# A gated cross-attention kernel: its first half regrouped into four phases a batch, with row-tiled transposes and another split of the PSUM reads

## The reference, cut to what matters

```python
xn   = layernorm(x)                                  # 32 x 112 x 256
qh   = split_heads(xn @ wq + bq)                     # 16 heads of 16
kh   = split_heads(ctx @ wk + bk);  vh = split_heads(ctx @ wv + bv)
attn = softmax(qh kh^T / 4 + mask * -1e9)            # 16 x 112 x 375
x    = x + tanh(g_xattn) * (merge(attn vh) @ wo + bo)
x    = x + tanh(g_ffn) * switch_attention(layernorm(x), ...)
```

## Time and profile before

| what | value |
|---|---|
| median of 3 runs | 1240.68 us (1239.48 to 1241.24) |
| profiled execution, its own time | 1238.06 us |
| its span, first to last instruction | 1236.3 us |
| PE, PEld busy | 96%, 77% of the span |
| DVE, ACT, POOL busy | 72%, 50%, 44% |
| DMA queue q1 | 71.1% of 16 engines' span |
| mean granted TensorE clock | 0.989 |

### The profile page before, as it was taken

One profiled execution on the slowest core, in us unless ns is written; L12 is line 12 of the kernel. 1 busy time (PEld: TensorE's weight loads), 2 busy tenths in 40 slices (PEclk: granted clock), 3 DMA queues, 4 the chain that ended last, 5 costly groups with the idle time before them and its releaser, 6 DMA issues. The chain is left out here.

```text
span 1236.3 us, 42159 instructions
## 1 busy us (share of the span) xinstructions
PE 1181.6 (96%) x16696; PEld 951.6 (77%) x16696; DVE 891.2 (72%) x2556; ACT 621.5 (50%) x1513; POOL 547.7 (44%) x821
## 2 busy tenths in 40 slices
PE   5799999999999999999879999999999999999975
PEld 4577777777777777777658888888888888888864
DVE  3577777777777777777666778777877877787752
ACT  3466666666666666666434444444444444444431
POOL 3476777777677777767610222122122212221210
PEclk9899999999999999999999999999999999999997
DMA  8898999788888778877316576666666665666663
GB/s 236 197 202 195 215 193 200 177 184 184 180 187 182 178 177 188 179 175 159 88 29 137 144 156 151 156 148 149 150 154 149 154 155 140 158 147 158 150 140 78
DMA packets 263011, 200.32 MB, mean 162 GB/s; under 512 B 195934, under 2 KB 243872, under 8 KB 258720
## 3 DMA queue, kind: packets, MB, share of 16 engines
q1 hardware_dynamic: 262816, 197.64, 71.1%
HBM read 125.49 MB, written 72.11 MB: 160 GB/s over the span
## 5 line engine op out<-in xcount | busy, mean ns | idle before, releaser
L899 POOL TENSOR_SCALAR shifted<-raw,neg_max 112x375 f32<-112x375 f32 x512 | 326.1, 645 | 164.9 <-DVE neg_max L781 121.1
L781 DVE CUSTOM_DVE_ANT_0 raw<-bank_s,maskb 112x375 f32<-112x375 f32 x512 | 266.6, 544 | 103.2 <-issue 88.1
L686 ACT ACTIVATE probsT<-bank_t 128x512 f32<-128x512 f32 (+3 forms) x512 | 189.2, 459 | 104.6 <-PE bank_t L460 104.6
L447 PE MATMUL bank_s<-K_stack,Q_stack 128*112 128x375 bf16 x512 | 151.1, 336 | 4.9 <-DVE neg_max L781 4.6
L460 PEld LDWEIGHTS bank_t<-ident,shifted 48*128 48x128 f32 (+1 forms) x3072 | 105.5, 139 | 28.0 <-issue 24.3
L203 POOL TENSOR_SCALAR var_eps<-moments 112x1 f32<-112x1 f32 x32 | 7.1, 223 | 261.1 <-DVE moments L199 260.9
L460 PE MATMUL bank_t<-ident,shifted 48*128 48x48 f32 (+1 forms) x3072 | 122.6, 226 | 0.2 <-issue 0.2
L1164 PE MATMUL bank_ab<-xnT,wq2T 128*128 128x224 f32 x512 | 109.5, 357 | 0.8 <-ACT qT L1365 0.6
L1164 PE MATMUL bank_ab<-xnT,wk2T 128*128 128x224 f32 x512 | 109.5, 357 | 0.0
L1476 DVE TENSOR_REDUCE max<-bank_s 112x4 f32<-112x448 f32 x128 | 78.8, 615 | 40.5 <-PE bank_s L1213 40.5
L1509 DVE COPY uT<-bank_g 64x192 f32<-64x192 f32 (+1 forms) x128 | 49.8, 389 | 80.6 <-PE bank_g L1263 79.3
(11 more groups left out here) (148 smaller groups left out, 2189.9 us busy)
## 6 DMA issues: line engine op xcount, KB each, us to landing
K_stack<-k_dram SPq DMA_DIRECT2D x64, 562.5 KB, 7.8
k_dram<-k_parts SPq DMA_DIRECT2D x32, 562.5 KB, 4.3
att_dram<-att_q SPq DMA_DIRECT2D x31, 511.0 KB, 3.3
att_th<-att_dram SPq DMA_DIRECT2D x31, 511.0 KB, 4.4
v_dram<-mv SPq DMA_DIRECT2D x32, 455.0 KB, 6.6
v<-v_dram SPq DMA_DIRECT2D x32, 455.0 KB, 4.5
K_stack<-k_dram SPq DMA_DIRECT2D x32, 375.0 KB, 9.3
Q_stack<-q_dram SPq DMA_DIRECT2D x64, 168.0 KB, 9.2
```

Of the source, the lines that this page charges most:

```text
L447: nc.tensor.matmul(bank_s[h % 2][0:S, 0:S2], Q_stack[:, p, h, :], K_stack[:, p, h, :], start=True, stop=True).then_inc(scores_ready, 1)
L686: act.activation(probsT[:, g % 2, first_u:end, lo:hi], bank_t[0:KP, bank, column:column + (end - first_u) * (hi - lo)].rearrange("p (u q) ...
L781: dve.tensor_tensor_reduce(raw[:, g % 2, j, :], bank_s[h % 2][0:S, 0:S2], c.maskb[:, :], -1.0, -LEAST, ALU.add, ALU.min, neg_max[:, g % 2, ...
L899: pool.tensor_scalar(shifted[:, g % 2, j, 0:S2], raw[:, g % 2, j, :], -1.0, neg_max[:, g % 2, j:j + 1], ALU.mult, ALU.add).then_inc(shift_ ...
```

## The change: what it does

- **Phases.** A batch is four phases of the same form: four scores with ordinary matmuls between them, then a `turn`, then a `weigh`. `turn` lies one group behind the scores and `weigh` one behind `turn`. Context and x are now turned for batch b+3, at the end of batch b.
- **Row-tiled turning.** The four small kinds of transposes are split as `turn` is: 64 rows each, half 0 to bank 0 and half 1 to bank 1 of `bank_ab` (`turn_halves`). They stand right behind a `turn`: `heads_back` behind the second, `heads_turn` behind the third, context and x behind the fourth. `xn`, `heads`, `xnT` and `outT` grow to 128 rows; POOL clears the tails once (`tails_set`). The heads come out in another order, so `wo` is loaded by four DMAs in that order.
- **Rests from PSUM.** ACT writes only the first part of k and q. DVE computes the rest straight from PSUM (`key_rest`, a half of k at a time, `query_rest`, two pieces), before PE may write that bank again. ACT makes the second key part in halves, POOL the third in halves. The scale 1/4 is put into `wq` once, in `prepare`.
- **Copies shared.** Context and turned x are copied out of PSUM by ACT (bank 0) and DVE (bank 1) at once.
- **Exchange.** Three query parts are stored, once; `Q_stack` is loaded by four DMAs. Queries are stored before keys. x is loaded one batch at a time.

The diff, cut to its core:

```diff
-STACKED = ((0, 3, 1), (3, 3, 2), (6, 2, 0))
+K_STACKED = ((0, 3, 0), (3, 3, 0), (6, 2, 0))
+Q_STACKED = ((0, 1, 2), (1, 2, 0), (3, 2, 0), (5, 3, 0))
...
+                sp.wait_ge(q_split, b + 1)
+                sp.dma_start(by_partition(q_dram[bass.ds(b, 1)]), q_parts[:, :, :, :]).then_inc(q_stored[p], 16)
+                sp.wait_ge(k_split, EC * (b + 1))
                 sp.dma_start(by_partition(k_dram[bass.ds(b, 1)]), k_parts[:, p, :, :, :]).then_inc(k_stored[p], 16)
...
+            def turn_halves(columns, width, src, f):
+                for r in range(2):
+                    rows = slice(r * HALF, (r + 1) * HALF)
+                    last = nc.tensor.transpose(bank_ab[0:f.stop - f.start, r, columns:columns + width], src[rows, f], c.ident[rows, rows])
+                return last
...
+            def body(b):
+                S_(b, 4, 5)
+                if b + 2 < B:
+                    keys(b + 2, 0, 0)
+                S_(b, 6)
+                if b + 2 < B:
+                    queries(b + 2)
...
+                S_(b, 7)
+                turn(b, 0, b == 0)
                 if back:
                     weigh(b - 1, 1 - p, NG - 1, False)
+                S_(b, 8, 9)
+                if b + 2 < B:
+                    keys(b + 2, 1, 0)
+                S_(b, 10, 11)
+                turn(b, 1, b == 0)
                 if back:
+                    if b + 2 < B:
+                        pe.wait_ge(k_rest_done, EC * (b + 3))
+                        pe.wait_ge(q_rest_done, EC * (b + 3))
...
                     heads_back(b - 1)
+                weigh(b, p, 0, b == 0)
+                S_(b, 12, 13)
+                if b + 1 < B:
...
                     values(1 - p, 0)
                     values(1 - p, 1).then_inc(va_ready, 1)
+                S_(b, 14, 15)
+                turn(b, 2, False)
+                if back:
...
+                    heads_turn(b - 1)
+                weigh(b, p, 1, False)
+                S_(b + 1, 0, 1)
+                if b + 1 < B:
...
+                    values(1 - p, 2).then_inc(vb_ready, 1)
                 else:
+                    open_proj(0)
+                S_(b + 1, 2)
+                if back:
+                    project(b - 1)
+                S_(b + 1, 3)
+                if b + 1 == B:
+                    open_proj(1)
+                turn(b, 3, False)
+                if b + 3 < B:
+                    turn_ctx(b + 3)
+                    turn_x(b + 3)
...
+                weigh(b, p, 2, False)
...
+            def key_rest(b, p, t, bank):
+                dve.wait_ge(k_copied, EC * b + t + 1)
...
+                dve.scalar_tensor_tensor(k_rest[:, t, :], bank_ab[:, bank, 0:S2], c.bk[:, t:t + 1], k_parts[:, p, 0, t, :],
+                                         ALU.add, ALU.subtract).then_inc(k_rest_done, 1)
...
+            def body(b):
+                score_max(b, b == 0, 4, 5)
+                if x_next < 0:
+                    moments_of(b + 3)
...
+                score_max(b, b == 0, 6)
+                if b + 2 < B:
+                    key_rest(b + 2, p, 0, 0)
+                score_max(b, b == 0, 7)
+                if b + 2 < B:
+                    query_rest(b + 2)
+                if x_next < 0:
+                    normalise_x(b + 3)
...
+                score_max(b, b == 0, 8, 9)
+                if b + 2 < B:
+                    split_rest(b + 2)
+                score_max(b, b == 0, 10)
+                if b + 2 < B:
+                    key_rest(b + 2, p, 1, 0)
+                score_max(b, b == 0, 11)
+                if back:
+                    normalise(b - 1)
+                score_max(b, b == 0, 12, 13)
+                if b + 1 < B:
                     value_copy(b + 1, 1 - p, 0)
+                score_max(b, b == 0, 14, 15)
+                if b + 1 < B:
+                    score_max(b + 1, False, 0, 1)
+                    value_copy(b + 1, 1 - p, 1)
+                    score_max(b + 1, False, 2)
+                if back:
                     residual(b - 1)
+                if b + 1 < B:
+                    score_max(b + 1, False, 3)
+                if b + 3 < B:
+                    ctx_copy(b + 3)
+                    x_copy(b + 3)
```

More of the change, by code:

```diff
@@ L323, in cross, with turned_ctx, ctx_half, turned_x @@
         block = ctx.enter_context(nc.Block())
[L325 to L333, removed]
+        def turned_ctx(r):
+            return bank_ab[:, r, 0:X_AT].rearrange("p (n s) -> p n s", s=HALF)
+        def ctx_half(b, r):
+            return ctxT[:, b % 2, :, :].rearrange("p e (k r s) -> p r (e k) s", r=2, s=HALF)[:, r]
+        def turned_x(r):
+            return bank_ab[:, r, X_AT:X_AT + EC * HALF].rearrange("p (e s) -> p e s", e=EC)
+        def x_half(r):
+            return xnT[:, :, r * HALF:(r + 1) * HALF]
         @block.sync
@@ L346, in exchange @@
[L346 to L348 removed]
+                if b >= 2:
                     sp.wait_ge(scores_ready, H * (b - 1))
                 sp.wait_ge(k_stored[p], 16 * i + 16)
[L351 removed]
+                for j, n, first in K_STACKED:
@@ L529, in open_proj @@
                 last.then_inc(o.proj_ready, 1)
-            def body(b, p, i, first, ahead, last):
-                back, front = not first, not last
-                S_ = lambda *hs: [scores(b, p, i, h, first) for h in hs]
-                if ahead:
-                    transposes(b + 2, i + 1, p)
-                S_(0, 1)
-                if back:
-                    weigh(b - 1, 1 - p, NG - 2, False)
-                    turn(b - 1, NG - 1, False)
-                S_(2, 3)
-                if ahead:
-                    keys(b + 2, p, 0)
-                S_(4)
+            def body(b):
+                p = b % 2
+                back = b > 0
+                S_ = lambda n, *hs: [scores(n, n % 2, n // 2, h, n == 0) for h in hs if n < B]
+                S_(b, 4, 5)
[4 more added lines that the diff above has]
+                    queries(b + 2)
+                elif b + 2 == B:
+                    open_gates(0)
+                S_(b, 7)
+                turn(b, 0, b == 0)
@@ L628, in _ @@
             pe.wait_ge(v_copied, 2)
-            batches(pe, body)
-            weigh(B - 1, 1, NG - 2, False)
-            open_proj(0)
-            turn(B - 1, NG - 1, False)
+            for h in range(G):
+                scores(0, 0, 0, h, True)
+            for b in range(B):
+                body(b)
             weigh(B - 1, 1, NG - 1, False)
-            pe.wait_ge(o.xt_copied, 2)
+            pe.wait_ge(x_done, B - 1)
             heads_back(B - 1)
-            open_proj(1)
             heads_turn(B - 1)
@@ L666, in query_copy, with key_copy @@
+            def key_copy(b, t, bank):
+                act.wait_ge(k_ready, EC * b + t + 1)
+                if t == 0 and b > 1:
+                    act.wait_ge(k_stored[b % 2], 16 * (b // 2))
+                act.activation(k_parts[:, b % 2, 0, t, :], bank_ab[:, bank, 0:S2], ACT.Identity, bias=c.bk[:, t:t + 1]).then_inc(k_copied, 1)
+            def query_copy(b):
                 act.wait_ge(q_ready, b + 1)
-                if not (isinstance(b, int) and b == 0):
+                if b > 0:
@@ new lines, in out_copy, with open_x_copy @@
+                act.activation(outT[:, :, :].rearrange("p e (r s) -> p r e s", r=2),
+                               bank_ab[:, :, 0:EC * HALF].rearrange("p r (e s) -> p r e s", e=EC), ACT.Copy).then_inc(outT_copied, 1)
+            def open_x_copy(e):
+                act.wait_ge(o.xt_ready, e + 1)
+                for r, (lo, hi) in enumerate(HALVES):
+                    last = act.activation(o.xnT[:, :, e, lo:hi], bank_ab[:, r, X_AT:X_AT + EC * HALF].rearrange("p (e s) -> p e s", e=EC)[:, :, 0:hi - lo], ACT.Copy)
+                last.then_inc(o.xt_copied, 1)
@@ L869, in _ @@
             last_rank.then_inc(o.consts_done, 1)
+            dve.wait_ge(tails_set, 1)
             moments_of(0)
             normalise_x(0)
+            ctx_copy(0)
+            for t in range(EC):
+                key_rest(0, 0, t, t)
             dve.wait_ge(v_set, 1)
@@ L949, in _ @@
                     last_set.then_inc(v_set, 1)
-                key_rest(b, b)
+                for t in range(EC):
+                    key_third(b, b, t)
                 add_bias(b)
-            batches(pool, body)
+            inverse_deviation(2)
+            add_bias(2)
+            shift(0, 0, True)
+            for b in range(B):
+                body(b)
 def switch(nc, z, d, c):
```

442 lines of the change are left out of this document (213 added, 229 removed).

## The result

| what | before | after |
|---|---|---|
| median of 5 runs each | 1240.68 us (1239.48 to 1244.0) | 1248.54 us (1246.49 to 1252.55) |
| profiled span | 1236.3 us | 1246.8 us |
| PE, DVE, ACT, POOL busy | 96%, 72%, 50%, 44% | 94%, 75%, 46%, 43% |

The changed kernel is slower: 1.0062 of before (95% interval 1.0041 to 1.0082). The prediction was 1234, in a range that ended at 1248: wrong in sign, and just outside the range. The profiled execution before lies 2.6 under its median, the one after at its median; so the spans differ by 10.5, the medians by 7.9.

A forecast was written before the change was run, and what follows sets the result against it. PE was taken to bound the first half: 29 batches x (18.06 - 18.07) = 0, start +2, end -8, so -6 on 1238.06 gives 1232; the median lies 2.6 higher, so 1234 us, range 1217 to 1248.

The forecast's parts named there:

- PE's own work: PE's list in a regular batch falls from 18.07 to 17.28 us if nothing waits, with transpose pairs at 0.064.
- The wait at `heads_back`: Second phase: PE waits 0.78 us a batch for DVE's key rest, reaching `heads_back` at 2.82 against 3.60.
- DVE starts score 8 after 0.50: First term of DVE's 3.60 us in the second phase: it starts 0.50 after PE starts score 8.
- POOL's exchange of one subtraction for another: POOL's work in each batch: 750 elements of one subtraction are swapped for 750 of another.
- nowhere else each batch: Sign of being right: PE idles 0.6 to 0.9 ahead of `heads_back` and at no other place in a batch.
- the forecast's own signs of being wrong: No hole ahead of `heads_back`, or holes ahead of scores or keys where copies, POOL's shifts or the stacks come late.
- Rival B: Second phase: POOL holds DVE in both split steps, wait 1.2, batch 18.48, +12 in batches, 1247 in all; chance 0.18.
- Rival A: Second phase: DVE quicker or POOL out of its way, wait is ACT's 0.45, batch 17.73, 1225 in all; chance 0.25.
- The start: Before the regular batches: keys stored behind queries delay a load 1 to 2 us, plus pipeline fill; +2 (0 to 4).
- a little: At the start: what filling the longer pipeline takes, counted within the +2 us.
- The end: Last two batches and tail of the first half: 5.8 and about 2.2 us saved, -8 (-3 to -11).

The follow-up runs named there:

- Moving the chain out: Changed kernel with DVE's split of the query rest put behind score 13 and the normalising of x behind score 15: 1237.56 us, 0.9984 of before.
- the dose: Changed kernel with two more casts of the query rest into an unread spare tile, ahead of DVE's split: 1287.83 us, 1.0393 of before.
- keys first: Changed kernel with only the store order of the first two batches turned back, keys ahead of queries: 1248.33 us, 1.0061 of before.
- the key rest first: Changed kernel with split and normalising later, second projection behind `heads_back`, first context copy and key stores earlier, and `key_rest` ahead of score 10: 1230.67 us, 0.9926 of before.

## Why the prediction was wrong

- **PE's own work** was right: pairs at 0.065, 17.27 without waits against 17.28.
- **The wait at `heads_back`** came out right by itself (0.76 against 0.78), but by luck, not by its terms. "DVE starts score 8 after 0.50" measured 0.91. Scores 8 and 9 took 0.94 as written, the split 0.80 instead of 0.95, score 10 0.47, the key rest 0.60 instead of 0.61, the reaction 0.05 instead of 0.13: 3.77 instead of 3.60 in the batch shown. PE got there later too, by about as much, since score 11 had waited; so the two errors cancel.
- **The step that failed** in the batch is that first term. I took the 0.50 of a DVE that is free, from a place in the kernel before, and did not go through what the new order puts ahead of score 8: the normalising, beside POOL's key third. I asked what POOL does to the split, but not to this; POOL's exchange of one subtraction for another was counted by its sum alone, and so as nothing. The "nowhere else each batch" failed with it: 0.27 at score 11, 0.07 at the keys (where the 0.07 comes from, no run shows). A hole ahead of scores, where POOL's work makes DVE late, was one of the forecast's own signs of being wrong. Moving the chain out gave 0.51 a batch back, the dose took 0.74.
- **Rival B**'s time came (1247), but by luck: it had +12 in the batches, where +6 came, and the rest came from the start and the switch. It named the right pair of engines, but the wrong instruction: in the changed kernel the split was quicker than in the forecast, its cast 0.27 in nearly all batches, and 0.50 as a rule only when POOL's or DVE's order ahead of it was changed.
- **Rival A's** floor is real, but lower than forecast. With the chain emptied the wait is 0.39 and a batch 17.82 (17.73 forecast), and the read of score 10 still stands ahead of the key rest. With that behind it too, DVE starts right behind ACT's copy and the wait is 0.26 (1.05 - 0.79) instead of 0.45. A batch doesn't gain by it, since the next bound stands close, at the values.
- **The start** was sized too low, +8.1 instead of +2. The forecast had the right cause for the load, keys stored behind queries. It put 1 to 2 on it; with the order turned back 3.3 came back. The first keys, late by 3.3 behind the moments of x, were missing, but putting them right alone brought only 0.6 at context 2. The further 3.1 up to the first regular batch are work, not holes: PE is busy for 21.04 of the 22.38 there, and for 17.54 of the 19.27 before. With the longer pipeline four more scores, one `turn`, one `weigh` and the turning of another context lie ahead of the first regular batch; the forecast's "a little" for this was too low, and the end is shorter in part for the same reason.
- **The end**: -6.6 against -8, within its bounds: the last two batches take 31.96 to the last `turn` (31 forecast, 36.8 before), the tail behind it 9.28 instead of 11.07. Its other side was not seen: with the projection gone from the tail, PE has holes there and the second half begins at a lower clock, +2.4 by the switch.

From the prediction's 1232 for a profiled execution to the 1248.5 that came: +6 in the start, +6 in the batches, +1.5 at the end, +3 behind the switch.

## What to carry to other kernels

When a change makes an engine's read a condition for PE, write down that engine's whole list from the last free moment on, and for each instruction what POOL does at that time; a duration from another place in the kernel doesn't hold there. Taking one instruction out of such a chain moves the neighbour's work onto the next one, so move them together, or test with a dose. And at the start, look at the order of the stores in a queue: here it put off the load behind them by 2.7.

## What the runs showed of the hardware

- DVE's normalising of 112x256 elements took 0.40 where POOL's shift was nearly over when it began, 0.52 and 0.61 beside a shift that ended 0.38 and 0.47 after its start (the run with the normalising moved, the run with POOL's third moved), and 1.44 in the changed kernel. There POOL's third key part began 0.43 behind it in most batches and went ahead of it all the same. In each of these but the first it ended about 0.14 behind the end of POOL's instruction. The cast of the query rest took 0.27 or 0.50, the subtraction behind it 0.58 or 0.65 (0.39 in the kernel before). The key rest, with one input from PSUM and one from SBUF, kept its 0.60 (597 to 605 ns in all 54), with POOL at work beside every one. The Trainium skill, SBUF — State Buffer, section Who interferes with whom, says that a VectorE instruction with two SBUF inputs or in a two-port mode and a GpSimd instruction that reads SBUF exclude each other, the later one waiting for the whole of the other. The trace agrees in that the normalising waited for the end of POOL's instruction, and in that the key rest, which isn't of that kind, lost nothing. But by the profile's start times it wasn't always the later one that waited, and whether the normalising ran in a two-port mode no run shows.
- One kernel (keys first) has regular batches of 18.27 and of 18.78, by which of two instructions, POOL's shift or DVE's cast that by the profile starts 0.07 behind it, holds the other.
- In the changed kernel PE's granted clock fell in the tail, behind holes of 0.92 and 0.76, to the lower of its two levels (1.2 GHz): the last projection of the first half already takes 2.05 instead of 1.03, the first of the second half 2.02 instead of 1.09. In all eight profiles without the second projection in the tail the switch was slow (6.2 to 7.4 between two projections there), in all four with it, the kernel before among them, it was not (4.9). But in two of the four, the kernel before and that of the key rest first, the projection itself ran at the lower level (3.52 and 3.46 instead of 1.97), and the clock was back by the switch. So the filling does not always hold the clock, and what else decides stays open.
- With the dose, PE's hole ahead of `heads_back`, counted from the end of the drain, grew from some 0.55 to between 1.1 and 1.4 in nearly every batch. Behind five of these the clock fell, behind the others of the same size it did not. In the changed kernel, with 0.55 there and 1.0 once, it fell nowhere between 100 and 600 us.
